# Six pairs ahead of the first gates with copied up products, and the second sequence's statistics behind the first sequence's gates

## The chip, the cores and the metric

One core of a Trainium2 chip runs the whole kernel in one launch. The metric is the device time of that launch in microseconds, lower is better, as the median of several runs.

## The reference

Eight sequences of 512 tokens go through a small language-model tower of width 128. A token's embedding is a gathered fine half and a coarse half (a softmax over 64 gathered cluster logits times a table). Then a layer norm, a linear attention with decay and a gelu memory step, each added to the residual, a second layer norm, and a mixture of 64 experts of width 64, top 6 of a softmax router, with a capacity, plus two shared experts:

```python
hg = jnp.einsum('ecd,efd->ecf', expert_in, w_gate)
hu = jnp.einsum('ecd,efd->ecf', expert_in, w_up)
expert_out = jnp.einsum('ecf,edf->ecd', jax.nn.silu(hg) * hu, w_down)
```

The kernel computes every expert for every token and multiplies each hidden row by the token's gate, which is zero where the router did not choose the expert or its capacity is used up.

## The kernel before

Experts are taken two at a time, 33 pairs a sequence (pair 0 is the shared one), as 128 hidden rows by 512 tokens. For each pair TensorE (PE) makes a gate product and an up product (three float32r matmuls each, `x_hi` and `x_lo` being the split halves of the input, `L481` to `L483`) into one of two banks each (`bank_g`, `bank_u`). ScalarE (ACT) writes `silu(gate)` into a slot of `hid` (`L623`), VectorE (DVE) multiplies the slot by the up bank (`L881`, which frees that bank), GpSimd (POOL) multiplies it by the gate rows (`L1040`, pair 0 by a constant, `L1044`), and PE adds the down product to `bank_y` (`L467`; odd pairs in three float32r matmuls, `L461` to `L464`, for which ACT makes `hid_hi`, `L629`, and DVE `hid_lo`, `L887`). `hid` has six slots, so silu of pair p waits for the down product of pair p-6.

The next sequence's attention, norm and router are cut into stages, numbered by the pair behind which they stand (`PE_AT`, `DVE_AT`, `ACT_AT`, `POOL_AT`): `late` stages prepare sequence b+1, `early` ones the embedding of b+2. Every engine's order is written out by hand, and semaphores alone tie the engines. Some stages: 0 and 1 normalise and transpose `xn` (PE `L351`), 3 and 4 make y, 5 z and scores, 6 the state (PE `L378`), 7 the memory product (PE `L386`), 8 to 12 x2, its squares and `xn2` (PE `L396`), 23 the router product (PE `L419`), 24 to 29 its softmax and top 6 on DVE, 30 the transposed gates (PE `L427`), 31 the capacity count and `gates_t` (DVE `L828`, `L833`), which SyncE (SP) stores to memory and reads back as gate rows.

The first sequence has no predecessor: its stages run alone in a prologue, with transposes of the identity (`warm`, `L512`) put in where PE would idle. The prologue also splits the weights into hi and lo parts chunk by chunk (`split_hi` on ACT, `split_lo`, `L277`, on DVE; the table `CHUNKS` holds the places, and pairs 11 on need chunk 3, "up" in `later`). `AHEAD = 3` pairs of the first sequence have their gate and up products in the prologue: pairs 0 and 1 ahead of the transposed gates, pair 2 behind them. The embedding statistics of the second sequence (`bn1`, `mv1`, `L863` to `L873`) and its inverse deviation on POOL (`inv1`, `L1021`) stand amid the first sequence's router on DVE. From then on one function per engine (`pe_sequence` and its like) runs each sequence; the stages of the second sequence stand behind the pairs 0 to 32 of the first.

Of the kernel before, what the change touches and what calls it, by code (L numbers as in the profile page):

```python
# [45 lines left out]
LAG = 4  # L46
# [42 lines left out]
def build(nc, ids, table, coarse_w, square_w, small_cols, small_rows, gate_t, up_t, down_t, out):  # L89
    ctx = ExitStack()  # L90
    with ctx:
# [114 lines left out]

        def staging(b):
            return b.rearrange("p r s -> p (r s)")[:, 0:CHUNK * P].rearrange("p (c d) -> p c d", c=CHUNK)
# [42 lines left out]
        block = ctx.enter_context(nc.Block())  # L251

# [217 lines left out]
        def gate_up(pe, b, par, p):  # L470

            q = PAIRS * b + p
            if b == 0 and p % CHUNK == 0:
                for n in ("gate", "up"):
# [18 lines left out]
        def pe_sequence(pe, b, par, late, early):  # L493
            first = b == 0
            for p in range(PAIRS):
                if p >= AHEAD or not first:
                    gate_up(pe, b, par, p)
                if p >= LAG:
                    down(pe, b, par, p - LAG)
                elif not first:  # L500
# [3 lines left out]
                if late:  # L504
                    pe_late(pe, b + 1, 1 - par, p, early)
                if early:
                    pe_early(pe, b + 2, p)
# [7 lines left out]
        def _(pe):  # L515
# [37 lines left out]
            for p in range(PAIRS):  # L553
                if p == PE_AT["gates_t"]:
                    pe.wait_ge(sem("x3_hi"), 1)
                    pe.wait_ge(sem("x3_lo"), 1)
                    for k in range(AHEAD - 1):
                        gate_up(pe, 0, 0, k)
                    warm(pe, bank_y[1], WARM_GATES)
                pe_late(pe, 0, 0, p, False)  # L560
                if p == PE_AT["gates_t"]:
                    gate_up(pe, 0, 0, AHEAD - 1)
# [72 lines left out]

        def act_sequence(act, b, par, late, early):
            first = b == 0
            for p in range(PAIRS):
                if p == ACT_AT["ffn_t"] and not first:
                    act_copy_out(act, b - 1, 1 - par)  # L640
                if late:
                    act_late(act, b + 1, 1 - par, p)
                if early:
                    act_early(act, b + 2, p)
# [3 lines left out]
                if p >= SPLIT_LAG and is_split(p - SPLIT_LAG):  # L648
# [11 lines left out]
        def _(act):  # L660
# [9 lines left out]
            for p in range(PAIRS):  # L670
                act_late(act, 0, 0, p)
                act_early(act, 1, p - SHIFT, bank_y)
                split_hi(act, p)
                if p == DOWN_HI_AT:
# [4 lines left out]
                    act.activation(gelu_sig[:, :], sig[:, :], ACT.Gelu)  # L679
            sequences(act, lambda *a: act_sequence(act, *a))  # L680
# [202 lines left out]

        def dve_lo(dve, b, par, p):
# [10 lines left out]
        def dve_sequence(dve, b, par, late, early):  # L895
            first = b == 0
            for p in range(PAIRS):
                if p == DVE_AT["result"] and not first:
                    dve_out(dve, b - 1, 1 - par)
                if late:  # L900
                    dve_late(dve, b + 1, 1 - par, p)
                if early:
                    dve_early(dve, b + 2, par, p, b // 2 + 2)
                if first:
                    split_lo(dve, PAIRS + p)
                if p >= AHEAD - 1 or not first:
                    dve_up(dve, b, par, p)
                if p >= SPLIT_LAG and is_split(p - SPLIT_LAG):
# [5 lines left out]
        def _(dve):  # L914
# [58 lines left out]
            for p in range(PAIRS):  # L973
                if p == DVE_AT["taken"]:
                    dve_up(dve, 0, 0, 0)
                dve_late(dve, 0, 0, p)
                if p == DVE_AT["taken"]:
                    dve_up(dve, 0, 0, 1)
                dve_early(dve, 1, 1, p - SHIFT, 1, bank_y)
                split_lo(dve, p)  # L980
            sequences(dve, lambda *a: dve_sequence(dve, *a))
# [42 lines left out]
        def pool_sequence(pool, b, par, late, early):  # L1024
            for p in range(PAIRS):
                if late:
                    pool_late(pool, b + 1, 1 - par, p)
                if early:
                    pool_early(pool, b + 2, p)
# [18 lines left out]
        def _(pool):  # L1048
# [74 lines left out]
```

## Time and profile before

| | |
|---|---|
| median of 3 runs | 718.56 us (717.55 to 718.6) |
| span of the profiled execution, first to last instruction | 716.0 us |
| PE busy | 692.8 us, 97% |
| DVE, POOL, ACT busy | 523.4, 466.5, 350.6 us |

The profiled execution's own time is known by its span alone; 1.6 to 2.6 us lie between that span and the runs' times. The page's slices show PE at 9 tenths or more from the ninth slice on, and below that in the first eight. A time in a row counts from the span's start. PE's matmuls overlap at their ends: the distance between two starts, not one's length, is what a matmul costs.

### The profile page before, as it was taken

Reading aid. Unit: us, or ns where it says so; the run is one execution under the profiler, and the core shown is the slowest. Engines: PE = TensorE matmul, PEld = TensorE weight load, DVE = VectorE, ACT = ScalarE, POOL = GpSimd, SP = SyncE. Lnnn points to the kernel's source line nnn. Section 1 sums busy time; section 2 is a strip of 40 time slices with the busy share of each in tenths; the row PEclk is TensorE's granted clock in tenths of the full one; section 3 lists DMA queues with packets and bytes.
Section 4 is the critical chain, followed back from the end, with each engine's and each line's share of the span. In section 5 each row is a group of like instructions: output and inputs, shape, how many; then the busy total and the mean of one; then the engine's idle time right before and its main releaser. Section 6 shows DMA issues by size and latency. Waiting matters only on the chain.

```text
span 716.0 us, 9975 instructions
## 1 busy us (share of the span) xinstructions
PE 692.8 (97%) x3133; PEld 524.7 (73%) x3133; DVE 523.4 (73%) x1074; ACT 350.6 (49%) x609; POOL 466.5 (65%) x345
## 2 busy tenths in 40 slices
PE   7788899999999999999999999999999999999998
PEld 7666677777777777777777777777777777777775
DVE  5677686987768867887769877788678766674444
ACT  3543455446454374445553474544745435534432
POOL 5035477776677767685676776676775656676664
PEclk9999999999999999999999999999999999999999
DMA  5504232243323333333333433333333433334431
GB/s 204 226 1 128 71 118 104 85 133 105 111 106 114 114 108 99 120 113 102 118 103 101 128 103 103 118 110 109 114 105 102 125 103 105 115 112 124 138 123 60
DMA packets 48869, 80.17 MB, mean 112 GB/s; under 512 B 9520, under 2 KB 13744, under 8 KB 48816
## 3 DMA queue, kind: packets, MB, share of 16 engines
q1 hardware_dynamic: 47792, 77.44, 33.4%
q0 software_dynamic: 1024, 2.10, 1.2%
q8 instruction: 25, 0.41, 0.2%
q14 instruction: 28, 0.23, 0.1%
HBM read 76.35 MB, written 3.15 MB: 111 GB/s over the span
## 4 chain that ended last, share of the span: by engine, by line
PE 88%; DVE 4%; issue 3%; POOL 2%; ACT 1%; DVEq 0%; POOLq 0%
PE bank_y L467 16%; PE bank_g L481 8%; PE bank_g L482 8%; PE bank_g L483 8%; PE bank_u L483 8%; PE bank_u L481 8%; PE bank_u L482 8%; PE bank_y L464 4%; PE bank_y L462 4%; PE bank_y L461 4%; POOL hid L1040 1%; PE bank_f L408 1%; PE bank_f L386 1%; PE bank_f L402 1%; PE bank_f L445 1%
## 5 line engine op out<-in xcount | busy, mean ns | idle before, releaser
L1040 POOL TENSOR_TENSOR hid<-hid,gate_rows 128x512 f32<-128x512 f32 x256 | 374.2, 1470 | 195.4 <-DVE hid L881 193.0
L623 ACT ACTIVATE hid<-bank_g 128x512 f32<-128x512 f32 x264 | 156.6, 599 | 264.4 <-PE bank_g L483 261.8
L881 DVE TENSOR_TENSOR hid<-hid,bank_u 128x512 f32<-128x512 f32 x264 | 178.7, 681 | 128.3 <-PE bank_u L483 78.2
L481 PE MATMUL bank_g<-x_hi,gate_hi 128*128 128x512 f32 x264 | 142.9, 541 | 0.0
L467 PE MATMUL bank_y<-hid,w_down 128*128 128x512 f32 x272 | 138.7, 591 | 0.0
L887 DVE TENSOR_TENSOR hid_lo<-hid,hid_hi 128x512 fp32r<-128x512 f32 x128 | 110.2, 861 | 2.4 <-ACT hid_hi L629 2.4
L482 PE MATMUL bank_g<-x_hi,gate_lo 128*128 128x512 f32 x264 | 104.5, 396 | 0.0
L483 PE MATMUL bank_g<-x_lo,gate_hi 128*128 128x512 f32 x264 | 104.5, 396 | 0.0
L481 PE MATMUL bank_u<-x_hi,up_hi 128*128 128x512 f32 x264 | 103.9, 393 | 0.1
L483 PE MATMUL bank_u<-x_lo,up_hi 128*128 128x512 f32 x264 | 103.8, 393 | 0.0
L482 PE MATMUL bank_u<-x_hi,up_lo 128*128 128x512 f32 x264 | 103.8, 393 | 0.0
L629 ACT ACTIVATE hid_hi<-hid 128x512 fp32r<-128x512 f32 x128 | 80.3, 628 | 5.5 <-POOL hid L1040 4.8
L481 PEld LDWEIGHTS bank_g<-x_hi,gate_hi 128*128 128x128 f32 x264 | 50.1, 190 | 24.1 <-issue 19.2
L482 PEld LDWEIGHTS bank_g<-x_hi,gate_lo 128*128 128x128 f32 x264 | 50.2, 190 | 23.9 <-issue 19.2
L467 PEld LDWEIGHTS bank_y<-hid,w_down 128*128 128x128 f32 x272 | 51.1, 188 | 11.3
L481 PEld LDWEIGHTS bank_u<-x_hi,up_hi 128*128 128x128 f32 x264 | 49.8, 189 | 12.4 <-DVE hid L881 0.6
L482 PEld LDWEIGHTS bank_u<-x_hi,up_lo 128*128 128x128 f32 x264 | 49.8, 189 | 11.8
L483 PEld LDWEIGHTS bank_g<-x_lo,gate_hi 128*128 128x128 f32 x264 | 49.7, 188 | 11.6
L483 PEld LDWEIGHTS bank_u<-x_lo,up_hi 128*128 128x128 f32 x264 | 49.8, 189 | 11.1
L461 PE MATMUL bank_y<-hid_hi,down_hi 128*128 128x512 f32 x128 | 51.3, 401 | 0.0
L464 PE MATMUL bank_y<-hid_lo,down_hi 128*128 128x512 f32 x128 | 50.8, 397 | 0.0
L462 PE MATMUL bank_y<-hid_hi,down_lo 128*128 128x512 f32 x128 | 50.6, 395 | 0.0
(209 smaller groups left out, 857.1 us busy)
## 6 DMA issues: line engine op xcount, KB each, us to landing
gate_rows<-gates_dram SPq DMA_DIRECT2D x512, 128.0 KB, 2.9
w_down<-down_t_dram SPq DMA_DIRECT2D x3, 704.0 KB, 14.5
out_dram<-later SPq DMA_DIRECT2D x7, 256.0 KB, 3.1
hid<-gate_t_dram SPq DMA_DIRECT2D x2, 704.0 KB, 5.8
gates_dram<-gates_t SPq DMA_DIRECT2D x8, 128.0 KB, 2.2
gate_rows<-up_t_dram SPq DMA_DIRECT2D x1, 704.0 KB, 5.7
later<-up_t_dram SPq DMA_DIRECT2D x1, 704.0 KB, 9.9
raw<-gate_t_dram SPq DMA_DIRECT2D x1, 704.0 KB, 11.0
```

Source lines behind the costliest of these rows:

```text
L461: pe.matmul(y, down_hi[:, j, :], hid_hi[:, k, :], start=False, stop=False)
L462: pe.matmul(y, down_lo[:, j, :], hid_hi[:, k, :], start=False, stop=False)
L464: pe.matmul(y, down_hi[:, j, :], hid_lo[:, k, :], start=False, stop=False).then_inc(sem("down_done"), 1)
L467: pe.matmul(y, w_down[:, p, :], hid[:, slot(par, p), :], start=(p == 0), stop=(p == PAIRS - 1)).then_inc(sem("down_done"), 1)
L481: pe.matmul(o, w_hi[name][:, p, :], x3_hi[par][:, :], start=True, stop=False)
L482: pe.matmul(o, w_lo[name][:, p, :], x3_hi[par][:, :], start=False, stop=False)
L483: pe.matmul(o, w_hi[name][:, p, :], x3_lo[par][:, :], start=False, stop=True).then_inc(sem("pe_" + name), 1)
L623: act.activation(hid[:, slot(par, p), :], bank_g[(p + par) % 2][:, :], ACT.Silu).then_inc(sem("silu"), 1)
L629: act.activation(hid_hi[:, (p // 2) % SPLIT_RING, :], hid[:, slot(par, p), :], ACT.Copy)\
L881: dve.tensor_tensor(hid[:, s, :], hid[:, s, :], bank_u[(p + par) % 2][:, :], ALU.mult)\
L887: dve.tensor_tensor(hid_lo[:, k, :], hid[:, slot(par, p), :], hid_hi[:, k, :].bitcast(F32), ALU.subtract)\
L1040: pool.tensor_tensor(hid[:, s, :], hid[:, s, :], gate_rows[:, row, :], ALU.mult)\
```

## The change

`AHEAD` goes to 6. The gate and up products of pairs 0 to 5 now stand ahead of the first sequence's pair loop: 0 and 1 as before, then 14 warm transposes in place of 20, pair 2, the gate product of pair 3, the transposed gates, and then the up product of pair 3 and the pairs 4 and 5. The 6 warm transposes behind the gates are gone. Since only two up banks exist, ACT copies each of these six up products to SBUF buffers that are free then (`u_copy`), and DVE multiplies silu by the copy (`dve_first_product`). The copy of pair 0 stands ahead of the router's exponential on ACT. The second sequence's `bn1` and `mv1` move on DVE from amid the router to behind the first `gates_t`; POOL gathers the third sequence's rows ahead of `inv1` and no longer behind it. The pair loop of the first sequence begins at pair 6, and three tables say which stages, down products and hi/lo splits stand behind which pair; three chunk splits on DVE move.

```diff
-AHEAD = 3
-WARM = {1: 8, 3: 12, 5: 9, 6: 7, 7: 36, 12: 3, 13: 4, 17: 24, PE_AT["gates_t"]: 6}
-WARM_START, WARM_PREP, WARM_EXP, WARM_COARSE, WARM_GATES = 20, (2, 9), 4, 26, 20
+AHEAD = 6
+FIRST_STAGES = {6: (0, 1, 2), 7: (3,), 8: (4,), 9: (5,), 10: (6,), 11: (7,), 12: (8, 9), 13: (10,), 14: (11,), 15: (12,),
+                16: (13,), 17: (14, 15), 18: (16,), 19: (17,), 20: (18,), 21: (19,), 22: (20,), 23: (21, 22), 24: (23,),
+                25: (24, 25), 26: (26,), 27: (27,), 28: (28,), 29: (29,), 30: (30,), 31: (31,), 32: (32,)}
+FIRST_DOWNS = {6: (0,), 7: (), 8: (1, 2), 9: (3, 4), 10: (5, 6)}
+FIRST_HI = {6: (1,), 7: (), 8: (3,), 9: (5,), 10: (7,)}
+FIRST_PRODUCTS = {0: (3,), 2: (4, 5)}
+WARM = {1: 8, 3: 12, 5: 9, 6: 7, 7: 36, 12: 3, 13: 4, 17: 24}
+WARM_START, WARM_PREP, WARM_EXP, WARM_COARSE, WARM_GATES = 20, (2, 9), 4, 26, 14
...
-          ("up", CHUNK, "later", None, 5, PAIRS + 5),
-          ("gate", 2 * CHUNK, "own0", None, 5, PAIRS + 9),
-          ("up", 2 * CHUNK, "own1", None, 7, PAIRS + 12))
+          ("up", CHUNK, "later", None, 5, PAIRS + 8),
+          ("gate", 2 * CHUNK, "own0", None, 5, PAIRS + 11),
+          ("up", 2 * CHUNK, "own1", None, 7, PAIRS + 13))
...
-            for name, banks, freed in (("gate", bank_g, "silu"), ("up", bank_u, "up_used")):
+            for name, banks, freed in (("gate", bank_g, "silu"),
+                                       ("up", bank_u, "u_copied" if q - 2 < AHEAD else "up_used")):
...
+        def act_copy_up(act, p):
+
+            act.wait_ge(sem("pe_up"), p + 1)
+            if p == AHEAD - 1:
+                act.wait_ge(sem("pe_coarse"), 2)
+            act.activation(u_copy[p], bank_u[p % 2][:, :], ACT.Copy).then_inc(sem("u_copied"), 1)
...
+        def dve_first_product(dve, p):
+
+            dve.wait_ge(sem("silu"), p + 1)
+            dve.wait_ge(sem("u_copied"), p + 1)
+            s = slot(0, p)
+            dve.tensor_tensor(hid[:, s, :], hid[:, s, :], u_copy[p], ALU.mult).then_inc(sem("up_used"), 1)
...
-                pool_early(pool, 1, p - SHIFT)
             for t in range(TILES):
                 gather(pool, 2, 0, t)
+            pool_early(pool, 1, POOL_AT["inv1"])
             sequences(pool, lambda *a: pool_sequence(pool, *a))
```

PE around the first sequence's transposed gates (`L427` before, `L444` in the change); gate products write `bank_g`, up products `bank_u`. Before:

```order
L512 MATMUL bank_y<-ident 128x128 x20
L427 MATMUL bank_f<-ident,turns 128x128 x4
L481 MATMUL bank_g<-x_hi,gate_hi 128x512
L482 MATMUL bank_g<-x_hi,gate_lo 128x512
L483 MATMUL bank_g<-x_lo,gate_hi 128x512
L481 MATMUL bank_u<-x_hi,up_hi 128x512
L482 MATMUL bank_u<-x_hi,up_lo 128x512
L483 MATMUL bank_u<-x_lo,up_hi 128x512
L512 MATMUL bank_y<-ident 128x128 x6
L351 MATMUL bank_f<-ident,xn 128x128 x4
```

The same place in the change:

```order
L536 MATMUL bank_y<-ident 128x128 x14
L501 MATMUL bank_g<-x_hi,gate_hi 128x512
L502 MATMUL bank_g<-x_hi,gate_lo 128x512
L503 MATMUL bank_g<-x_lo,gate_hi 128x512
L501 MATMUL bank_u<-x_hi,up_hi 128x512
L502 MATMUL bank_u<-x_hi,up_lo 128x512
L503 MATMUL bank_u<-x_lo,up_hi 128x512
L501 MATMUL bank_g<-x_hi,gate_hi 128x512
L502 MATMUL bank_g<-x_hi,gate_lo 128x512
L503 MATMUL bank_g<-x_lo,gate_hi 128x512
L444 MATMUL bank_f<-ident,turns 128x128 x4
L501 MATMUL bank_u<-x_hi,up_hi 128x512
```

Pair 2 and half of pair 3 have moved ahead of the transposed gates.

DVE from the second sequence's embedding (`L858`) into the first sequence's router (`L779` to `L789`), before:

```order
L858 TENSOR_TENSOR emb<-bank_y,soft 128x4x64
L863 BN_STATS bn<-emb 128x6 x4
L779 TENSOR_TENSOR turns<-bank_f,rows 128x256
L783 TENSOR_REDUCE rstat<-turns 128x4
L785 TENSOR_TENSOR turns<-turns,rstat 128x256
L868 BN_AGGR mv<-bn 128x2 x4
L872 TENSOR_SCALAR var<-mv 128x4
L873 TENSOR_SCALAR var<-mv 128x4
L789 TENSOR_REDUCE rstat<-turns 128x4
```

In the change the router stands there alone, and DVE has this behind the last router step (`L935` is `dve_first_product`, `L874` and `L879` the capacity count and `gates_t`, `L743` stage 0 of the second sequence):

```order
L935 TENSOR_TENSOR hid<-hid,shared 128x512
L874 SCALAR_TENSOR_TENSOR taken<-ones_row,bank_f 64x512
L879 SCALAR_TENSOR_TENSOR gates_t<-taken,bank_f 64x512
L909 BN_STATS bn<-emb 128x6 x4
L914 BN_AGGR mv<-bn 128x2 x4
L918 TENSOR_SCALAR var<-mv 128x4
L919 TENSOR_SCALAR var<-mv 128x4
L935 TENSOR_TENSOR hid<-hid,shared 128x512 x2
L743 TENSOR_SCALAR xn<-emb,mv,inv 128x128 x4
```

The eight statistics instructions and the two on the variance now follow `gates_t`; POOL's `inv1` waits for them and stands ahead of POOL's work on pair 0.

DVE around the first of the three moved chunk splits (`L277` before, `L294` in the change; `L716` and `L718` are stage 4, `L881` a product). Before:

```order
L716 TENSOR_TENSOR vo_y_lo<-bank_f,vo_y_hi 128x512
L718 TENSOR_TENSOR turns<-bank_f,decay_out 128x384
L881 TENSOR_TENSOR hid<-hid,bank_u 128x512
L703 TENSOR_SCALAR x<-emb,mv,inv 128x128 x4
L708 TENSOR_SCALAR shared<-xn,decay_cols 128x384
L277 TENSOR_TENSOR up_lo<-later,up_hi 128x1408
L881 TENSOR_TENSOR hid<-hid,bank_u 128x512
L887 TENSOR_TENSOR hid_lo<-hid,hid_hi 128x512
```

In the change (`L927` a product, the first that of pair 7; `L940` the lo half, here of pair 3):

```order
L927 TENSOR_TENSOR hid<-hid,bank_u 128x512
L762 TENSOR_TENSOR vo_y_lo<-bank_f,vo_y_hi 128x512
L764 TENSOR_TENSOR turns<-bank_f,decay_out 128x384
L294 TENSOR_TENSOR up_lo<-later,up_hi 128x1408
L927 TENSOR_TENSOR hid<-hid,bank_u 128x512
L940 TENSOR_TENSOR hid_lo<-hid,hid_hi 128x512
```

Stage 4 and the split now stand in one row ahead of the lo half of pair 3.

## Rows read from the trace of the kernel before

**Rows 1.** Windows: two stretches; length, busy us of each engine, clock, DMA.

```profile
60.70:64.10 3.40, 3.40 (x10) 2.66 (x9) 1.97 (x3) 1.52 (x3) 0.36 (x1) 0.50 0.50 153
74.40:77.80 3.40, 3.40 (x11) 3.01 (x12) 1.58 (x4) 0.50 (x2) 0.36 (x2) 0.50 0.17 62
```

**Rows 2.** Timeline of PE: start, us, what, count, idle ahead and its releaser.

```profile
50.78 2.35 PE L512 MATMUL bank_y<-ident 128*128 128x128 f32 x20
55.27 0.65 PE L427 MATMUL bank_f<-ident,turns 128*128 128x128 f32 x4 [2.14 <-DVE turns L819]
...
57.16 0.82 PE L512 MATMUL bank_y<-ident 128*128 128x128 f32 x6
59.89 0.66 PE L351 MATMUL bank_f<-ident,xn 128*128 128x128 f32 x4 [1.92 <-DVE xn L697]
...
74.36 1.62 PE L378 MATMUL bank_f<-z,shared 128*128 128x128 f32 x6 [2.24 <-issue]
```

**Rows 3.** The chain that ended last, in order of time: start, us, what.

```profile
61.16 0.43 PE bank_g L483
...
90.93 0.67 DVE xn L746 x3
...
97.04 0.86 PE bank_y L467 x2
...
99.60 0.23 PE bank_g L483
```

**Rows 4.** Timeline of DVE from the router to the pair loop.

```profile
48.24 0.87 DVE L863 BATCH_NORM_STATS2 bn<-emb 128x6 f32<-128x128 f32 x4
49.03 0.41 DVE L779 TENSOR_TENSOR turns<-bank_f,rows 128x256 f32<-128x256 f32 x1
...
50.84 0.42 DVE L789 TENSOR_REDUCE rstat<-turns 128x4 f32<-128x256 f32 x1
...
54.79 0.42 DVE L819 TENSOR_TENSOR turns<-turns 128x256 f32<-128x256 f32 x1
...
57.21 0.69 DVE L833 SCALAR_TENSOR_TENSOR gates_t<-taken,bank_f 64x512 f32<-64x512 f32 x1
...
61.82 0.68 DVE L881 TENSOR_TENSOR hid<-hid,bank_u 128x512 f32<-128x512 f32 x1
```

**Rows 5.** Timeline of ACT at the router's exponential.

```profile
50.38 0.42 ACT L607 ACTIVATE turns<-turns 128x256 f32<-128x256 f32 x1 [3.23 <-DVE turns L785]
50.82 1.28 ACT L623 ACT_TABLE_LOAD   x1
52.12 1.08 ACT L623 ACTIVATE hid<-bank_g 128x512 f32<-128x512 f32 x2
```

**Rows 6.** Timeline of POOL at the same place.

```profile
51.00 1.64 POOL L1021 TENSOR_TENSOR inv<-var,neg_half 128x8 f32<-128x8 f32 x1 [6.83 <-DVE var L873]
...
57.65 1.53 POOL L1044 TENSOR_SCALAR hid<-hid 128x512 f32<-128x512 f32 x1
```

**Rows 7.** Timeline of DVE in the first pairs.

```profile
65.72 1.15 DVE L887 TENSOR_TENSOR hid_lo<-hid,hid_hi 128x512 fp32r<-128x512 f32 x1 [2.06 <-ACT hid_hi L629]
66.80 0.68 DVE L716 TENSOR_TENSOR vo_y_lo<-bank_f,vo_y_hi 128x512 fp32r<-128x512 f32 x1
67.40 0.54 DVE L718 TENSOR_TENSOR turns<-bank_f,decay_out 128x384 f32<-128x384 f32 x1
...
70.78 1.61 DVE L277 TENSOR_TENSOR up_lo<-later,up_hi 128x1408 fp32r<-128x1408 f32 x1
```

**Rows 8.** Timeline of PE: four stages of the second sequence.

```profile
80.12 0.39 PE L386 MATMUL bank_f<-z,shared 128*128 128x128 f32 x2
...
91.70 0.61 PE L396 MATMUL bank_f<-ident,xn 128*128 128x128 f32 x4
...
119.71 1.00 PE L419 MATMUL bank_f<-cols,xn_t 128*128 128x64 f32 x8
...
135.82 0.60 PE L427 MATMUL bank_f<-ident,turns 128*128 128x128 f32 x4
```

More of the change, by code:

```diff
@@ L251, in build, with stages @@
         block = ctx.enter_context(nc.Block())
+        def stages(b, p):
+            if b:
+                return (p,)
+            return FIRST_STAGES.get(p, ())
         def alone(eng, name):
@@ L497, in pe_sequence @@
                     gate_up(pe, b, par, p)
-                if p >= LAG:
+                if first:
+                    for k in FIRST_DOWNS.get(p, (p - LAG,) if p > AHEAD else ()):
+                        down(pe, b, par, k)
+                elif p >= LAG:
                     down(pe, b, par, p - LAG)
-                elif not first:
+                else:
                     down(pe, b - 1, 1 - par, p - LAG + PAIRS)
@@ L503, in pe_sequence @@
                     pe_out(pe, b - 1)
[L504 to L507, printed above, removed]
+                for at in stages(b, p):
+                    if late:
+                        pe_late(pe, b + 1, 1 - par, at, early)
+                    if early:
+                        pe_early(pe, b + 2, at)
         def warm(pe, bank, count):
@@ L647, in act_sequence @@
                 act_silu(act, b, par, p)
-                if p >= SPLIT_LAG and is_split(p - SPLIT_LAG):
+                if first:
+                    for k in FIRST_HI.get(p, (p - SPLIT_LAG,)):
+                        if is_split(k):
+                            act_hi(act, b, par, k)
+                elif p >= SPLIT_LAG and is_split(p - SPLIT_LAG):
                     act_hi(act, b, par, p - SPLIT_LAG)
@@ L896, in dve_sequence @@
             first = b == 0
-            for p in range(PAIRS):
+            for p in range(AHEAD if first else 0, PAIRS):
                 if p == DVE_AT["result"] and not first:
                     dve_out(dve, b - 1, 1 - par)
[L900 to L903, printed above, removed]
+                for at in stages(b, p):
+                    if late:
+                        dve_late(dve, b + 1, 1 - par, at)
+                    if early:
+                        dve_early(dve, b + 2, par, at, b // 2 + 2)
+                    if first:
+                        for k in FIRST_PRODUCTS.get(at, ()):
+                            dve_first_product(dve, k)
                 if first:
                     split_lo(dve, PAIRS + p)
-                if p >= AHEAD - 1 or not first:
-                    dve_up(dve, b, par, p)
-                if p >= SPLIT_LAG and is_split(p - SPLIT_LAG):
+                dve_up(dve, b, par, p)
+                if first:
+                    for k in FIRST_HI.get(p, (p - SPLIT_LAG,)):
+                        if is_split(k):
+                            dve_lo(dve, b, par, k)
+                elif p >= SPLIT_LAG and is_split(p - SPLIT_LAG):
                     dve_lo(dve, b, par, p - SPLIT_LAG)
@@ L1025, in pool_sequence @@
             for p in range(PAIRS):
-                if late:
-                    pool_late(pool, b + 1, 1 - par, p)
+                for at in stages(b, p):
+                    if late:
+                        pool_late(pool, b + 1, 1 - par, at)
+                    if early:
+                        pool_early(pool, b + 2, at)
                 if early:
-                    pool_early(pool, b + 2, p)
                     if p in GATHER_AT and b:
```

46 lines of the change are left out of this document (32 added, 14 removed).

## The prediction

> **What bounds the kernel now.** I read the page first: PE is busy 97% of the span, and its slices are full from the ninth on. What PE loses it loses early, and since it has the same matmuls to do afterwards, what is saved or lost early shows at the end one for one. Next the timeline of PE over the prologue's end, for every stretch without pairs in it. Around the first gates PE has two holes [rows 2]. From 50.78, when pair 1 is issued, to 55.27 it has only 20 warm transposes and a wait of 2.14 us for the router's last step on DVE: 4.5 us. From 57.16 to 59.89 it has 6 warm transposes and a wait of 1.92 for the second sequence's `xn`: 2.7 us. A third wait of 2.24 us stands ahead of the state product. Then the clock: it is granted at 0.50, which is 1.2 of 2.4 GHz, in two stretches of 3.4 us, one right behind the second hole, one right behind the third [rows 1]. In them a matmul costs 0.43 us and not 0.23 [rows 3], so each stretch loses 3.4 x (1 - 0.23/0.43) = 1.6 us. Sum of before's early losses: 4.5 + 2.7 + 2.2 + 2 x 1.6 = **12.6 us**. The change can at most win these.
>
> **The change, step by step,** in the time of before's trace. PE's own costs: 0.23 us a float32r matmul, so 1.38 a pair (gate and up) and 0.69 an odd down product, and 0.86 an even one [rows 3]; four transposes 0.41 (start of `L427` to the gap-free next matmul). No row shows the new copy on ACT; the nearest is silu, also 128x512 from a bank, two in 1.08, so 0.54 each [rows 5]. It may be as short as nothing where ACT is idle.
>
> Router. Before, the four `bn1` instructions stand ahead of the router's first step, 48.24 to 49.03 [rows 4]; they go, 0.8 us. But ACT now copies pair 0's up product ahead of the exponential. That product ends near 49.5 (one pair, 1.38, ahead of 50.78, and its tail), the copy near 50.2, so the exponential begins at 50.2 and not at 50.38 [rows 5]: 0.2 are won, not 0.8. `mv1` lay in the wait for the exponential (`L789` begins 0.04 behind its end [rows 4, 5]), so its removal wins nothing. The gates are ready at 55.0, not 55.2.
>
> Before the gates PE has 14 warm transposes, by 20 in 2.3 us **1.6 us**, then pair 2's gate product, which waits for silu 0: exponential to 50.6, table load 1.28, silu 0.6 gives 52.5 [rows 5], a wait of **0.1**. Nine matmuls, to 54.6; then a wait of **0.4** for the gates, transposes to 55.45, and 21 matmuls of pairs 3 to 6, to 60.3. ACT's silu and copy, 1.08 a pair, hide beside PE's 1.38.
>
> Down product of pair 0. The moved statistics cost here. `gates_t` ended 2.63 behind the start of `L427` [rows 2, 4], so now at 57.7. Then `bn1` 0.87 and the aggregates behind it (0.7 taken, they are the shorter ones), 59.25; then POOL, whose queue holds `inv1`, 1.64, and behind it pair 0, 1.53 [rows 6]: 62.45. Queued behind POOL's wait is all of its pair work, and DVE's stage 0 waits for `inv1` too. PE stands from 60.3, **2.1 us**. Before, `inv1` was done by 52.7, off the path.
>
> Up product of pair 8. Down 0 and `xn`'s transposes end at 63.75, pair 7, y and pair 8's gate at 66.5. DVE had `x_lo` done 1.93 behind the start of `L351` [rows 2, 4], so now at 65.25; then it has the products of 4, 5 and 6, 0.6 apart: 67.05. The products of 0 to 5 now read two SBUF operands, where the old ones read a bank. An instruction with two SBUF operands that meets POOL's work took 1.15 [rows 7], against 0.68 of a product from a bank [rows 4]: with 0.47 more for two of them, 68.0. So PE waits 0.5 to 1.5. If the clock falls behind the 2.1 us, as it did behind 1.92 and 2.24, the 1.6 lost to it swallow most of that wait. I take **2.1** for both together (1.6 the one alone, 3.1 both in full).
>
> The row is one instance of that meeting. The Trainium skill, page "SBUF — State Buffer", section "SBUF: two separate sides", says of such a DVE instruction and of a GpSimd one that reads SBUF that the one that "starts first gets the pair for the whole instruction; the other fully blocks". By that rule each of the three products of this place could stand a whole POOL instruction.
>
> Down product of pair 3. Silu 7 waits for down 1's slot, then come 0.6 of silu, 0.6 of product 7, 1.06 of stage 4 (66.80 to 67.86), 1.55 of the moved chunk split, 0.6 of product 8, 0.65 of the lo half [rows 4, 7]: 5.1, and 5.6 with one meeting with POOL. PE has down 2, pair 9 and two thirds of down 3 meanwhile, 0.86 + 1.38 + 0.46 = 2.7. It waits 2.4 to 3.6, **2.9** taken, and the clock falls again, **1.6**. At down 7 the same pattern, shorter (state, product, lo half against 1.84 of PE): **0.5**.
>
> Later. The second sequence's stages now lie behind fewer pairs. From the memory product to `xn2`'s transposes PE had five pairs, 80.12 to 91.70 [rows 8], and `xn2` ended at 91.60 [rows 3]: just in time. Now there are four, 1.38 + 0.78 = 2.2 us less cover, of which the chain shrinks by at most the missing pair's product and lo half, 1.3. PE waits 0.9 to 2.2; **2.0** taken, since DVE also has two more chunk splits just ahead of it. From the router product to the transposed gates there were seven pairs, 119.71 to 135.82 [rows 8], now six; I don't know the slack from these rows, so 0 to 2.2, **1.2** taken.
>
> Sum of after's losses: 1.6 + 0.1 + 0.4 + 2.1 + 2.1 + 2.9 + 1.6 + 0.5 + 2.0 + 1.2 = **14.5 us**, against 12.6: **1.9 us slower**. The profiled span is 716.0, so 717.9 for the changed one; on the median, 718.56 + 1.9 = **720.5**. From the second sequence's own pairs on nothing is changed.
>
> **Rivals.** (a) The change wins nothing and loses nothing: the two later waits take their low ends, 0.9 and 0, since chains of stages are paced by the pairs between them. Then 14.5 - 2.3 = 12.2, a gain of 0.4: 718.2. For it: before, each such stage came just in time, as written by hand. Against it: `xn2` had no slack at all.
> (b) Faster, by the clock. It falls behind neither new hole, because PE is dense from 52.5 on but for them: 3.2 less (of which the wait at pair 8 takes back about 1), and with the low ends of (a) 12.2 - 2.2 = 10.0, a gain of 2.6: 716.0. It decides from the point where both holes stay below the 1.92 at which the clock fell before. I work them out at 2.1 and 2.9, so this is unlikely.
> (c) Slower still, by DVE and POOL meeting. If each of the three products and two of the lo halves waits a whole POOL instruction (0.47 by the row, up to the 1.15 of the whole), 5 x 0.5 = 2.5 more, of which half meets waits that are counted: 1.3 more, 721.8. By that rule of the Trainium skill, page "SBUF — State Buffer", section "SBUF: two separate sides", the time would go this way.
> (d) The change does not do what it says: pair 2 could not start ahead of the gates because silu 0 comes too late. Silu 0 would have to end behind 55; by rows 5 it ends at 52.5. Time as before.
>
> **How the numbers follow.** A measurement of this kernel tells a change from none at about 0.2%, 1.44 us: faster is below 717.1, slower above 720.0. Chances: forecast 0.50, with its own range 719.4 to 721.8 and a tenth of it below 720.0; (a) 0.25, within; (b) 0.12, of which 0.11 faster; (c) 0.10, slower; (d) 0.03, within. That gives slower 0.55, within 0.34, faster 0.11. The range reaches down to the middle of (a) and (b), 717.3, and up to 722.4, where (c) and the high ends of the waits at pairs 3 and 8 lie.
>
> **What would show it.** In the changed trace: the first hole shrunk to 14 warm transposes and less than 1 us of wait; the first even down product waiting some 2 us for POOL's pair 0, which starts right behind `inv1`; the lo product of pair 3 waiting some 3 us for DVE's lo half, with the chunk split ahead of it; two stretches at clock 0.50 between 60 and 85 us; and idle time ahead of `xn2`'s transposes, or of a gate product that waits for silu near them. The pair loop of the first sequence should be some 5 us early around pair 12 without the clock's falls and 2 with them, and late by pair 33. I am wrong if PE's waits in that stretch sum to less than before's, above all if the late ones are missing or the clock stays at 1.00.

## The result, and the profile after

The changed kernel took 721.41 us (median of 7 runs, 719.73 to 722.52), the kernel before beside it 717.92 us (7 runs, 716.48 to 718.6): a ratio of 1.005, 95% interval 1.0039 to 1.0061. It is 3.5 us slower. The forecast was 720.5, 1.9 to 2.6 us slower depending on which median of before it is set against, with a range of 717.3 to 722.4: the side and the range hold, the size is too small.

The profiled execution of the change spans 719.6 us, against 716.0. First its TensorE (PE), in the timeline: start, us, what, count, and in brackets the idle time ahead and what ended it. Left out are most of the matmuls that waited for nothing.

```profile
49.36 0.47 PE L501 MATMUL bank_g<-x_hi,gate_hi 128*128 128x512 f32 x1
...
52.17 1.69 PE L536 MATMUL bank_y<-ident 128*128 128x128 f32 x14
53.87 0.50 PE L501 MATMUL bank_g<-x_hi,gate_hi 128*128 128x512 f32 x1
...
56.38 0.66 PE L444 MATMUL bank_f<-ident,turns 128*128 128x128 f32 x4 [0.15 <-DVE turns L865]
...
64.37 2.04 PE L484 MATMUL bank_y<-hid,w_down 128*128 128x512 f32 x2 [2.52 <-POOL hid L1109]
...
71.58 0.49 PE L501 MATMUL bank_u<-x_hi,up_hi 128*128 128x512 f32 x1 [1.15 <-DVE hid L927]
...
78.98 0.50 PE L481 MATMUL bank_y<-hid_lo,down_hi 128*128 128x512 f32 x1 [2.77 <-DVE hid_lo L940]
...
87.66 0.50 PE L481 MATMUL bank_y<-hid_lo,down_hi 128*128 128x512 f32 x1 [0.51 <-DVE hid_lo L940]
...
97.57 0.50 PE L501 MATMUL bank_g<-x_hi,gate_hi 128*128 128x512 f32 x1 [0.82 <-ACT hid L651]
...
100.72 0.66 PE L413 MATMUL bank_f<-ident,xn 128*128 128x128 f32 x4 [0.76 <-DVE xn L792]
...
132.74 0.51 PE L501 MATMUL bank_u<-x_hi,up_hi 128*128 128x512 f32 x1 [0.28 <-DVE hid L927]
...
143.47 0.80 PE L501 MATMUL bank_g<-x_hi,gate_hi 128*128 128x512 f32 x1
```

The first row is pair 0, the last pair 33 (the second sequence's first). The first hole, 4.5 us before [rows 2], is 1.7 of warm transposes now, and the second, 2.7, is gone. In their place stand eight waits. In the kernel before, the same two pairs begin here:

```profile
47.98 0.47 PE L481 MATMUL bank_g<-x_hi,gate_hi 128*128 128x512 f32 x1
...
140.18 0.80 PE L481 MATMUL bank_g<-x_hi,gate_hi 128*128 128x512 f32 x1
```

So from pair 0 to pair 33 PE needed 92.20 us before and 94.11 now, 1.91 more. Pair 0 itself came 1.38 later, though PE's work ahead of it is not changed, and 0.3 came behind pair 33: 3.6 in all. Of the 1.38, 0.34 is a longer wait for the first gathered rows (2.01 us, 1.66 before), and nearly all of the rest came at half clock behind it. The windows of the change (length, busy us of PE, weight loads, DVE, ACT and POOL, granted clock, DMA share, GB/s) show the clock at half between 12.9 and 19.7, where before had the full clock. It is at half again behind the first down product, and not behind the longest wait of all, the one that ends at 78.98:

```profile
12.90:16.30 3.40, 3.34 (x15) 2.85 (x14) 0.93 (x4) 1.76 (x2) 0.68 (x1) 0.50 1.01 412
16.30:19.70 3.40, 3.40 (x18) 3.40 (x18) 3.03 (x20) 1.38 (x1) 1.68 (x1) 0.51 1.02 407
64.10:67.50 3.40, 3.13 (x8) 1.97 (x9) 0.87 (x3) 0.20 (x1) 2.53 (x3) 0.52 0.68 199
75.90:79.40 3.50, 0.73 (x4) 0.38 (x3) 3.50 (x4) 0.00 (x0) 1.34 (x2) 1.00 0.57 182
79.00:83.00 4.00, 4.00 (x22) 3.23 (x23) 4.00 (x9) 2.34 (x6) 2.14 (x2) 1.00 0.22 67
```

The fourth of these windows shows what PE waits for there: PE is busy for 0.73 of 3.50 us, VectorE (DVE) for all 3.50. Its timeline from the gates to that lo half, and one chunk split at the late waits (start, us, line, what, count; the bracket as above):

```profile
58.32 0.69 DVE L879 SCALAR_TENSOR_TENSOR gates_t<-taken,bank_f 64x512 f32<-64x512 f32 x1
58.93 0.86 DVE L909 BATCH_NORM_STATS2 bn<-emb 128x6 f32<-128x128 f32 x4
...
60.50 1.29 DVE L935 TENSOR_TENSOR hid<-hid,shared 128x512 f32<-128x512 f32 x2
62.75 1.62 DVE L743 TENSOR_SCALAR xn<-emb,mv,inv 128x128 f32<-128x128 f32 x4 [0.96 <-POOL inv L1084]
64.30 0.67 DVE L935 TENSOR_TENSOR hid<-hid,shared 128x512 f32<-128x512 f32 x1
67.94 0.69 DVE L758 TENSOR_TENSOR x_lo<-bank_f,x_hi 128x512 fp32r<-128x512 f32 x1 [2.97 <-ACT x_hi L608]
...
69.14 1.78 DVE L935 TENSOR_TENSOR hid<-hid,z 128x512 f32<-128x512 f32 x1
70.85 0.67 DVE L927 TENSOR_TENSOR hid<-hid,bank_u 128x512 f32<-128x512 f32 x1
...
73.96 0.69 DVE L927 TENSOR_TENSOR hid<-hid,bank_u 128x512 f32<-128x512 f32 x1 [1.36 <-ACT hid L651]
...
75.63 2.09 DVE L294 TENSOR_TENSOR up_lo<-later,up_hi 128x1408 fp32r<-128x1408 f32 x1
...
78.25 0.68 DVE L940 TENSOR_TENSOR hid_lo<-hid,hid_hi 128x512 fp32r<-128x512 f32 x1
...
94.28 1.62 DVE L294 TENSOR_TENSOR up_lo<-raw,up_hi 128x1408 fp32r<-128x1408 f32 x1
```

DVE is not busy all the way: it waits 2.97 us for `x_hi` and 1.36 for silu of pair 7. From 73.96 to the end of the lo half, at 78.93, its row has no gap, and that row is what PE waits for.

And POOL: `inv1`, pair 0, pairs 1 and 2, pair 3, and one at the late waits.

```profile
60.68 2.04 POOL L1084 TENSOR_TENSOR inv<-var,neg_half 128x8 f32<-128x8 f32 x1 [10.24 <-DVE var L919]
62.72 1.51 POOL L1109 TENSOR_SCALAR hid<-hid 128x512 f32<-128x512 f32 x1
65.09 2.49 POOL L1105 TENSOR_TENSOR hid<-hid,gate_rows 128x512 f32<-128x512 f32 x2 [0.87 <-DVE hid L935]
...
68.63 1.75 POOL L1105 TENSOR_TENSOR hid<-hid,gate_rows 128x512 f32<-128x512 f32 x1 [1.04 <-DMA gate_rows<-gates_dram]
...
94.44 2.58 POOL L1105 TENSOR_TENSOR hid<-hid,gate_rows 128x512 f32<-128x512 f32 x1 [1.88 <-DVE hid L927]
```

### The profile page after: what moved, and what is told of

Read it like the earlier page. It is cut to its first block, busy times and chain, and to the rows that moved or that the text cites. A ratio compares the mean times of both kernels' runs of the same rounds, so it can differ in the third digit from the quotient of the medians.

```text
span 719.6 us, 9958 instructions
## 1 busy us (share of the span) xinstructions
PE 695.2 (97%) x3121; PEld 523.6 (73%) x3121; DVE 524.1 (73%) x1074; ACT 354.1 (49%) x615; POOL 467.5 (65%) x345
## 4 chain that ended last, share of the span: by engine, by line
PE 88%; issue 4%; DVE 3%; POOL 2%; ACT 1%; DMA 1%; SPq 0%; DVEq 0%; POOLq 0%; ACTq 0%
PE bank_y L484 16%; PE bank_g L501 8%; PE bank_u L501 8%; PE bank_g L502 8%; PE bank_g L503 8%; PE bank_u L503 8%; PE bank_u L502 8%; PE bank_y L481 4%; PE bank_y L479 4%; PE bank_y L478 4%; PE bank_f L395 1%; PE bank_f L403 1%; PE bank_f L425 1%; PE bank_u L536 1%; PE bank_f L462 1%
## 5 line engine op out<-in xcount | busy, mean ns | idle before, releaser
L927 DVE TENSOR_TENSOR hid<-hid,bank_u 128x512 f32<-128x512 f32 x258 | 174.6, 681 | 125.1 <-PE bank_u L503 73.8
L501 PE MATMUL bank_g<-x_hi,gate_hi 128*128 128x512 f32 x264 | 141.0, 534 | 0.8 <-ACT hid L651 0.8
L940 DVE TENSOR_TENSOR hid_lo<-hid,hid_hi 128x512 fp32r<-128x512 f32 x128 | 108.7, 849 | 0.4 <-ACT hid_hi L657 0.4
```

The lines of the kernel that those rows point to most:

```text
L501: pe.matmul(o, w_hi[name][:, p, :], x3_hi[par][:, :], start=True, stop=False)
L927: dve.tensor_tensor(hid[:, s, :], hid[:, s, :], bank_u[(p + par) % 2][:, :], ALU.mult)\
L940: dve.tensor_tensor(hid_lo[:, k, :], hid[:, slot(par, p), :], hid_hi[:, k, :].bitcast(F32), ALU.subtract)\
```

## The experiments

How many stretches at half clock an execution has differs from run to run of one kernel. Each run has its span and its mean granted clock, and a stretch of 3.4 us at 0.50 takes 3.4 x 0.5 / 716 = 0.0024 off that mean: 0.998 or 0.997 is one such stretch, 0.995 two, 0.993 three. So beside the medians the table has the spans of the runs that had one, and of those that had none. All these kernels but the first carry 14 more warm transposes in the prologue, "three" and "six" are the pairs ahead, "early" statistics stand amid the router as before, "late" ones behind the first `gates_t` as in the change.

| kernel | median us (runs) | ratio to before, 95% | span with one stretch | with none |
|---|---|---|---|---|
| before, unchanged | 717.72 to 717.88 (81) | 1 | 714.5 to 715.3 | |
| three early, `p_before` | 718.14 (12) | 1.000 (0.999 to 1.0009) | 714.7 to 714.9 | |
| six late, `p_after` | 721.68 (6) | 1.0053 (1.0038 to 1.0068) | 718.8 (one run) | |
| six early, `p_six_early` | 719.64 (12) | 1.0028 (1.0018 to 1.0039) | 716.5 to 716.8 | |
| three late, `p_three_late` | 718.16 (11) | 1.0008 (1.0 to 1.0017) | none such, 716.0 to 716.5 with two | |
| three early, split moved, `p_three_split` | 715.25 (11) | 0.997 (0.996 to 0.9981) | 713.2 to 714.7 | |
| six early, split moved, `p_six_split` | 717.09 (12) | 0.9989 (0.9978 to 1.0001) | 715.2 to 715.5 | 713.7 to 713.8 |
| six early, late splits, `p_six_own` | 717.98 (12) | 1.0002 (0.9989 to 1.0016) | 715.2 to 715.3 | 713.7 to 713.8 |
| six early, both, `p_six_both` | 715.44 (11) | 0.9966 (0.9955 to 0.9977) | 713.5 to 713.8 | 712.3 to 712.5 |
| six late, both, `p_after_both` | 716.25 (12) | 0.9986 (0.9975 to 0.9996) | 714.0 to 714.5 | 713.8 |
| six late, POOL's order, `p_after_pool` | 719.98 (8) | 1.0036 (1.0023 to 1.005) | 717.8 to 718.3 | 717.0 |
| six early, both, products moved, `p_six_all` | 713.50 (6) | 0.9946 (0.9932 to 0.9959) | none such | 711.5 to 712.1 |
| six late, everything, `p_after_all` | 714.04 (6) | 0.9956 (0.9942 to 0.9971) | 713.6 | 712.1 to 712.3 |

### Is it the clock ahead of pair 0?

```diff
-WARM_START, WARM_PREP, WARM_EXP, WARM_COARSE, WARM_GATES = 20, (2, 9), 4, 26, 20
+WARM_START, WARM_PREP, WARM_EXP, WARM_COARSE, WARM_GATES = 20, (2, 23), 4, 26, 20
```

The kernel before with this (`p_before`):

> The kernel before with 14 more warm transposes (1.6 us) in the prologue, where TensorE waits for the first gathered rows (1.66 us of wait in the profile of before, 2.01 in the profile of the change). In the change's profile the clock fell to 0.50 right behind that wait, from 12.9 to some 19.6, and its pair 0 started 1.38 us later than before's (49.36 to 47.98), although the change touches nothing there. Theory A (the fall is a matter of when the row numbers arrive, in either kernel): with the wait filled the clock stays at 1.00 ahead of pair 0 here, the time is that of before's profile, 716.0 of span, or up to 0.7 us below before's median. Theory B (something of the change lengthens its prologue): this kernel runs as before, and the next one keeps 1.4 us behind it ahead of pair 0.

The change with it (`WARM_GATES` 14 in both of its lines; `p_after`):

> The changed kernel with the same 14 warm transposes. Theory A: pair 0 starts at 48.0, within 0.3 of the one before it here, from pair 0 to pair 33 TensorE needs 94.1 us as in the change's profile against 92.2 before, so this kernel is 1.9 to 2.2 us (0.3%) slower than the one above, and not 3.5. Theory B: 3.5 us slower, 1.4 of it ahead of pair 0.

Measured: no change to before (1.000), and the change is 3.5 us behind `p_before`, as without the warm transposes. Of theory A one half held: in both profiles the clock was full until pair 0, which began at 48.16 and 48.33. But `p_after` then fell to half at 48.2, with no idle time above 0.98 us in the 28 us ahead of it, and it was at half for most of the 3.5 us behind each of its long waits, which end at 64.65 and 78.10 (windows as above):

```profile
48.20:51.60 3.40, 3.40 (x11) 2.72 (x10) 1.61 (x5) 0.32 (x1) 0.95 (x1) 0.51 0.14 39
64.60:68.10 3.50, 3.45 (x10) 2.33 (x11) 1.08 (x3) 1.06 (x3) 2.98 (x3) 0.59 0.58 199
78.10:81.90 3.80, 3.80 (x14) 3.00 (x15) 3.46 (x7) 1.12 (x2) 1.95 (x2) 0.60 0.18 68
```

From pair 0 to pair 33 it took 95.88 us, against 92.33 of `p_before`: 3.55 more. So the 1.38 ahead of pair 0 was no part of the change, and the 1.91 behind it is not the change's size: between these two pairs the clock fell twice in the profiles of before and `p_before`, once in the change's, and three times in `p_after`'s. With one stretch each, before (714.5 to 715.3) and the change (718.5 in its first seven runs, 718.8 here) lie some 3.5 to 4 us apart.

### Statistics and pairs, one without the other

The statistics back in their old place, with six pairs ahead (`p_six_early`); the last part is on POOL:

```diff
-                if p - SHIFT < DVE_AT["bn1"]:
-                    dve_early(dve, 1, 1, p - SHIFT, 1, bank_y)
+                dve_early(dve, 1, 1, p - SHIFT, 1, bank_y)
...
-            dve_early(dve, 1, 1, DVE_AT["bn1"], 1, bank_y)
-            dve_early(dve, 1, 1, DVE_AT["mv1"], 1, bank_y)
...
+                pool_early(pool, 1, p - SHIFT)
...
-            pool_early(pool, 1, POOL_AT["inv1"])
```

> The changed kernel with the same warm transposes and with the second sequence's statistics back amid the first router, inv1 at its old place on POOL. Theory S (the moved statistics cost it): the gates come 0.8 us later, but POOL has pair 0 done by 60, so the 2.5 us wait of the first down product and the stretch at half clock behind it (1.5) go, and the later waits go along with TensorE: 94.1 - 4.2 + 0.8 = 90.7 us from pair 0 to pair 33, 3.4 us faster than the kernel above and 1.5 faster than the first. Rival C (the crowd behind six pairs ahead): what is won at the first down product comes back at the waits behind it (second sequence's xn, gate rows, up product of pair 8, lo half of pair 3), so 93 to 94 us, within 1 us of the kernel above.

The opposite edit on the kernel before (`p_three_late`):

> The kernel before with the same warm transposes, three pairs ahead, but with the second sequence's statistics behind the first gates_t and inv1 behind the third sequence's gathers, as in the change. Theory S: the gates come 0.8 us earlier, but xn waits for bn1 0.87, aggregates 0.7, inv1 1.6 to 2.0, so its transposes start 2.1 to 2.9 us later than before's 59.89, and the kernel is 2 to 3 us slower than the first. Rival C (the statistics' place is free, six pairs make the loss): up to 0.8 us faster than the first.

Measured: undoing the statistics won 2.0 us of the change's 3.5 and not 3.4; six pairs with early statistics are still slower than before. And moving them with three pairs cost nothing (718.16 to 718.14; 0.6 by the ratios, within their intervals), where a loss of 2 to 3 us was expected, the router's 0.8 already taken off. So six pairs alone, with the tables that go with them, cost 1.5 us (719.64 to 718.14), the statistics alone nothing, and both together 3.5. The hole that was to cost them is there, in PE's timeline of `p_three_late`:

```profile
63.21 1.12 PE L351 MATMUL bank_f<-ident,xn 128*128 128x128 f32 x4 [5.71 <-DVE xn L697]
...
76.42 0.91 PE L378 MATMUL bank_f<-z,shared 128*128 128x128 f32 x6
```

In `p_before` the same two are:

```profile
60.07 0.66 PE L351 MATMUL bank_f<-ident,xn 128*128 128x128 f32 x4 [1.91 <-DVE xn L697]
...
74.64 1.61 PE L378 MATMUL bank_f<-z,shared 128*128 128x128 f32 x6 [2.25 <-issue]
```

The transposes of `xn` come 3.1 us later and the state product, behind pair 6, only 1.8, because it no longer waits; pair 33 then starts 0.07 us later after pair 0. (The clock was at half there from 48 to 51 too, but PE's wait for the gates, 2.12 us in `p_before`, is gone.) What sets the state product is DVE's row up to its scores (`L725`), which starts at the lo half of pair 1. In `p_before` DVE waited 2.11 us there for `hid_hi`, which ACT makes from POOL's pair 1; in `p_three_late` that lo half comes only 1.7 later, at 67.59, and without a wait:

```profile
65.86 1.28 DVE L887 TENSOR_TENSOR hid_lo<-hid,hid_hi 128x512 fp32r<-128x512 f32 x1 [2.11 <-ACT hid_hi L629]
...
71.06 1.61 DVE L277 TENSOR_TENSOR up_lo<-later,up_hi 128x1408 fp32r<-128x1408 f32 x1
...
73.79 0.74 DVE L725 TENSOR_TENSOR shared<-bank_f,decay_mask 128x256 f32<-128x256 f32 x2
```

From 65.86 to 74.5 this row has no gap. In `p_six_early` the first down product waited for nothing, as expected. But PE then met DVE where it had met it in the change, for longer:

```profile
66.71 0.50 PE L501 MATMUL bank_u<-x_hi,up_hi 128*128 128x512 f32 x1 [1.18 <-DVE hid L927]
...
74.60 0.50 PE L481 MATMUL bank_y<-hid_lo,down_hi 128*128 128x512 f32 x1 [3.26 <-DVE hid_lo L940]
```

That gave a new theory: from the first gates to about pair 10 DVE sets the pace, and PE's waits there are one account, not several.

### Work taken out of VectorE's row

One number moves the first chunk split, 1.6 us of DVE, from behind pair 5 to the prologue, between the first `x3` and `x_lo`, where DVE had waited 1.87 us for ACT (`p_three_split`; with six pairs from `PAIRS + 8`, `p_six_split`):

```diff
-          ("up", CHUNK, "later", None, 5, PAIRS + 5),
+          ("up", CHUNK, "later", None, 5, 20),
```

> The kernel before (three pairs ahead, statistics amid the router, 14 more warm transposes in the prologue) with one thing moved: the chunk split that pairs 11 on need (up_lo from later, 1.6 to 2.1 us on VectorE) stands in the prologue, behind the first x3 and ahead of x_lo, where VectorE waited 1.87 us for ScalarE. Theory D (from the first gates to pair 10 VectorE has more to do than TensorE, so what TensorE wins or loses there is given back at the next wait for VectorE; that is why a hole of 5.7 us at xn cost nothing in the run with three pairs and late statistics): the wait ahead of the state product falls from 2.25 to some 0.7, the time by 1.5 us, to 716.3. Rival L (TensorE's waits add up one for one, each with a cause of its own): the state product waits for its own chain, at most 0.5 us change.

> Six pairs ahead, statistics amid the router, the same warm transposes, and the same chunk split in the prologue. In the run without the split moved the first down product waited for nothing, as expected, but the lo half of pair 3 waited 3.26 us where it was 2.77, and pair 33 came only 1.7 us earlier than with late statistics. Theory D: that wait falls to 0.8 to 1.2, the time by 1.5 to 2 us (more where a stretch at half clock behind it goes too), from 719.6 to some 717.8. Rival P (POOL, which then has eight pairs in a row, 12.7 us, sets the pace): the wait moves to pairs 5 and 7 and the time stays within 0.5.

Two more splits moved back by two pairs (`p_six_own`), and all three moves together (`p_six_both`):

```diff
-          ("gate", 2 * CHUNK, "own0", None, 5, PAIRS + 11),
-          ("up", 2 * CHUNK, "own1", None, 7, PAIRS + 13))
+          ("gate", 2 * CHUNK, "own0", None, 5, PAIRS + 13),
+          ("up", 2 * CHUNK, "own1", None, 7, PAIRS + 15))
```

> Six pairs ahead, statistics amid the router, the same warm transposes, and the two other chunk splits (gate_lo and up_lo from raw, 2.7 and 1.6 us on VectorE) two pairs later, behind pairs 13 and 15 and no longer 11 and 13. Theory T (the late waits are VectorE's too: the split at pair 11 holds up the residual, its squares, and so the exponential with its two table loads on ScalarE): the gate product's wait for silu at pair 15 (0.82) goes, that of xn2's transposes (0.77) halves, 1.2 to 1.8 us less, 718.1. Rival F (the second sequence's stages lie behind fewer pairs, whatever VectorE does between): both waits stay, 719.6.

> Both moves of the splits together with six pairs ahead and statistics amid the router. Theories D and T: the gains add, 3.0 to 3.5 us less than without (719.6), so 716.1 to 716.6, 1.2 to 1.7 below the kernel before. Rivals L, P, F: within 0.5 of 719.6; if only one of D and T holds, near 718.

Measured, in the medians: 2.9 us won by the one number with three pairs and 2.5 with six, where 1.5 to 2 were expected; 1.7 by the late splits; 4.2 by both. By the ratios it is 2.2, 2.8, 1.9 and 4.5. L, P and F fall; the times go with D and T. In `p_three_split` the split fits its place, and pair 0 starts as before (48.19 to 48.16):

```profile
45.45 1.62 DVE L277 TENSOR_TENSOR up_lo<-later,up_hi 128x1408 fp32r<-128x1408 f32 x1
47.40 0.69 DVE L774 TENSOR_TENSOR x_lo<-bank_f,x_hi 128x512 fp32r<-128x512 f32 x1 [0.33 <-ACT x_hi L604]
```

and PE's waits for `xn`, 1.91, and for the state product, 2.25, are these:

```profile
60.11 0.66 PE L351 MATMUL bank_f<-ident,xn 128*128 128x128 f32 x4 [0.56 <-DVE xn L697]
...
73.22 0.91 PE L378 MATMUL bank_f<-z,shared 128*128 128x128 f32 x6 [0.91 <-issue]
```

The first is not shorter by the split: `xn` ends where it did, and PE came to it later, since in this execution the clock was at half from 56.5 on. That shows how waits and clock stand in for each other. The state product's wait is shorter by 1.3, and the stretch behind it is gone; the products of `vo_y` (`L368`), ahead of it, now wait 0.65 for DVE. With one stretch each, the spans of these kernels with and without the split moved lie about 1.0 (three pairs) and 1.3 us (six) apart, so of what the medians show a third (three pairs) to a half (six) is DVE's directly, and I put the rest down to the clock. In `p_six_split` the wait for the lo half of pair 3 fell from 3.26 to 1.85, less far than the 0.8 to 1.2 expected. In `p_six_own` the gate product's wait for silu was gone, and `xn2`'s transposes waited 0.35, not 0.77.

### The changed kernel's own order

The statistics late again, with the three splits moved (`p_after_both`):

> The changed kernel, statistics behind gates_t, with the same warm transposes and both moves of the splits. So far: late against early statistics 2.0 us with the splits as in the change (721.68 to 719.64), the two moves 4.2 us with early statistics (719.64 to 715.44). Theory S (the moved statistics cost the first down product its wait, whatever VectorE does later): the gap of 2 stays, 721.7 - 4.2 = 717.5, and the first down product still waits 2.5 us. Theory D (what is lost at the first down product comes back where TensorE waits for VectorE next): the wait at the lo half of pair 3 shrinks by what the first one cost, as did the wait at the state product with three pairs, and the time is 715.4 to 716.4.

Late, splits as in the change, and only POOL's order exchanged (`p_after_pool`; the two lines move behind POOL's work on pair 0 of the first sequence):

```diff
+                    if b == 0:
+                        pool_early(pool, 1, POOL_AT["inv1"])
...
-            pool_early(pool, 1, POOL_AT["inv1"])
```

> The changed kernel with the same warm transposes and one exchange on POOL: pair 0 ahead of inv1, so that it waits for its product and no longer for inv1. The first down product's wait of 2.55 us then goes, since POOL can be done with pair 0 by some 58.5. Theory S: xn's transposes, right behind, then wait 0.7 to 1.7 us for xn, so 0.9 to 1.8 us are won, 720 to 720.8. Theory D: the wait at the lo half of pair 3 (2.77) grows by what is won, so under 0.5 us: 721.3 to 721.7.

Early, splits moved, and the products of pairs 4 and 5 ahead of `x_lo` (`p_six_all`); then the same with late statistics and POOL's exchange (`p_after_all`):

```diff
-FIRST_PRODUCTS = {0: (3,), 2: (4, 5)}
+FIRST_PRODUCTS = {0: (3, 4, 5)}
```

> Six pairs ahead, statistics amid the router, both moves of the splits, and the products of pairs 4 and 5 ahead of x_lo on VectorE (it waits there 1.60 us for x_hi) and no longer behind it. The up product of pair 8 waited 1.18 us for VectorE, behind a product that took 1.79 beside POOL. If that wait is the order's, it goes, and with theory D the lo half of pair 3 comes earlier too: 0.5 to 1.2 us less than 715.44, 714.2 to 714.9. If the products only meet POOL at another place, 715.4.

> The changed kernel, statistics behind gates_t, with everything: both moves of the splits, the products of pairs 4 and 5 ahead of x_lo, and pair 0 ahead of inv1 on POOL. Theory D: no more than 0.5 us from the run above, 714.2 to 715.4, since the gates come 0.8 us earlier and xn 0.7 to 1.7 later. Theory S: 1 to 2 us behind it, 715.5 to 717.

Measured: late statistics cost 0.8 us with the splits moved by the medians (716.25 to 715.44), 1.4 by the ratios to the runs of before on the same chip, and 2.0 or 1.8 without. In `p_after_both` the first down product still waited 2.53, but the lo half of pair 3 only 0.75 (1.83 in `p_six_both`): 716.25 lies in D's range, and by the ratio between the two.

```profile
63.40 1.10 PE L484 MATMUL bank_y<-hid,w_down 128*128 128x512 f32 x2 [2.53 <-POOL hid L1109]
...
75.10 0.50 PE L481 MATMUL bank_y<-hid_lo,down_hi 128*128 128x512 f32 x1 [0.75 <-DVE hid_lo L940]
```

From pair 0 to pair 33 PE's waits sum to 4.9 us there and to 4.5 in `p_six_both`, and pair 33 starts 89.65 and 89.56 us behind pair 0, with one stretch in each: in these profiles nearly all of the 2.53 came back. POOL's exchange won 1.7 in the medians and 1.2 by the ratios, as S had it, though the intervals overlap; with one stretch each it is 0.5 to 1.0 (718.8, one run, to 717.8 to 718.3), between the two theories. Its profile shows both parts, the wait that moved to `xn` and the one that grew from 2.77:

```profile
62.98 0.66 PE L368 MATMUL bank_f<-ident,xn 128*128 128x128 f32 x4 [1.24 <-DVE xn L743]
...
68.28 0.50 PE L501 MATMUL bank_u<-x_hi,up_hi 128*128 128x512 f32 x1 [1.50 <-DVE hid L927]
...
76.15 0.49 PE L481 MATMUL bank_y<-hid_lo,down_hi 128*128 128x512 f32 x1 [3.23 <-DVE hid_lo L940]
```

The products won more than expected, 1.4 by the ratios and 1.9 in the medians (713.50 to 715.44) for at most 1.2. In `p_six_all` they took 0.68 each (at 61.29 and 61.89), in what was DVE's idle time, and PE's longest wait between pair 0 and pair 33 is below 1 us:

```profile
71.50 0.50 PE L481 MATMUL bank_y<-hid_lo,down_hi 128*128 128x512 f32 x1 [0.76 <-DVE hid_lo L940]
...
77.00 0.50 PE L481 MATMUL bank_y<-hid_lo,down_hi 128*128 128x512 f32 x1 [0.93 <-DVE hid_lo L940]
```

All six of its runs had a mean granted clock of 0.999 or 1.000, which no run of before had. With late statistics the best is 0.5 to 0.7 us behind it, about where D had it. `p_six_all` beats both kernels: 0.54% or 4 us below before, 7 to 8 us below the change. What three pairs ahead would give with all of this was not tried.

## Why the prediction was right, and where it was not

**Side.** Right, and for the reason given: at the places it named, the waits it put there are longer than the holes they replace. (The page's slices are at 9 tenths from the sixth on, not the ninth, the middle of 718.2 and 716.0 is 717.1, not 717.3, and the 3.6 at the top of the wait at pair 3 is not worked out; the forecast's sum uses none of them.)

**The waits, place by place** (forecast, then measured from where PE's next matmul could have started). Warm transposes 1.6, 1.7. Silu of pair 0: 0.1, 0. Gates 0.4, 0.3. First down product 2.1, 2.7. Up product of pair 8, without the clock, 0.5, 1.3. Lo half of pair 3: 2.9, 2.9. At down 7: 0.5, 0.7. Late waits, silu and `xn2`: 2.0, 1.9. Router product to gates: 1.2, 0.5, and not at the gates but at an up product. That is 11.3 forecast and 12.0 measured.

**The size.** The sum of after's losses was forecast at 14.5 us, two stretches at half clock among them, and from pair 0 to pair 33 the profile has 94.11 - (92.20 - 12.6) = 14.5. That they agree is chance: the execution had one stretch there (1.6 us: the down product, transposes and first gate matmul behind its wait take 3.08 us from 64.37 to 67.45, and 0.86 + 0.41 + 0.23 = 1.5 at full clock), so its waits come to 12.9. The 0.9 beyond the 12.0 lies in small gaps that I did not assign. So the step that failed is the waits' sum, with before's 12.6 - 3.2 = 9.4: 11.3 - 9.4 = 1.9 more by the forecast, 12.9 - 9.4 = 3.5 more by the profile, and 3.5 in the medians. Of the 1.6 between them, the mis-sized terms are the first down product (0.6), the up product of pair 8 (0.8) and the small gaps (0.9), less 0.7 of the last wait.

**First down product.** The mechanism is as told, pair 0 behind `inv1` on POOL; `p_six_early` and `p_after_pool` each take the wait away. It is longer chiefly because `inv1` took 2.04 beside the two products on DVE and not the 1.64 of [rows 6], beside router steps.

**Up product of pair 8.** I priced DVE and POOL meeting at 0.47 for two products, by the 1.15 of [rows 7]. One of them took 1.78, against the 0.67 of pair 3's, so it stood nearly a whole POOL instruction: POOL's ran from 68.63 to 70.38, and DVE's, issued at 69.14, ended at 70.92, 0.54 behind it. The rule of the Trainium skill, page "SBUF — State Buffer", section "SBUF: two separate sides", that of a DVE instruction with two SBUF operands and a GpSimd one that reads SBUF the one that starts second is blocked until the first has ended, says that. The trace agrees from the other side as well: POOL's instruction at 94.44 took 2.58 where two took 2.49, while a split of DVE's ran from 94.28 to 95.90; 95.90 + 1.25 = 97.15, and it ended at 97.02. The product of pair 6, which reads a bank, took 0.67 at 70.85 with POOL busy beside it. So the forecast's "each of the three products" was one too many, since only those of pairs 4 and 5 have both operands in SBUF; and of these two one was held up. (c) was the better price for that one; as an outcome it gave 721.8, close to what was measured, but only 0.8 us of the excess lies at this place. `p_six_all` shows that with the same operands another place in DVE's order avoids the meeting.

**"What is saved or lost early shows at the end one for one."** This first step of mine is wrong. Taken as a statement on the total it must hold, but I used it for each hole by itself. `p_three_late` has a hole of 5.71 for one of 1.91, and its time is the same; `p_six_early` took away a wait of 2.55 us at the first down product and won 2.0 at the end; late statistics cost 0, about 1 or 2 us depending on what DVE has to do behind them. I had worked out DVE's row ahead of the lo half of pair 3 (5.1 us, 5.6 with one meeting; it took 5.6, from silu 7 at 73.33) and did not ask what it means that the same row stands ahead of before's state product: DVE, 73% busy by the page, is the bound of that stretch, and PE, 97% busy, is not.

**Late waits.** Right in size, wrong in the main cause. I put them on fewer pairs behind the stages. `p_six_own` kept the stages and moved two splits: the wait for silu went, that of `xn2` halved. I had named the splits in half a sentence and given them no price.

**Clock.** Forecast at two stretches for each kernel. The runs of before have 1 to 4 (29 of 81 have one, 32 three), the change's seven 1 to 4 as well. Rival (b) put its deciding point at a hole of 1.92 us; but a wait of 2.77 was followed by half clock in `p_after` and by full clock in the change's profile. The hole's length alone doesn't decide, so that point was not one. Before's own rows had said so: behind its wait of 2.14 us [rows 2] the six matmuls of pair 2 took 0.25 us each, which is full clock. What holds is the coarse reading: of `p_six_all`, in whose profile all of PE's waits behind pair 0 are under 1 us, none of six runs had such a stretch. Of the two stretches that were to lie between 60 and 85 us, the change's profile has one and `p_after`'s two. Pair 12 began 1.3 us early in the change's profile (40.11 us behind pair 0, 41.39 before) where 2 were forecast with the clock's falls, and pair 33 came late, as forecast.

**(d)** is out: pair 2 starts at 53.87 without a wait.

## What to carry to other kernels

Where a mostly busy engine waits several times in one stretch, look for one dense row of another engine behind all these waits; then closing a hole on the first engine may only make the next wait longer: here 2.5 to 3.8 us of a wait were worth 0 to 2.0 us at the end. The test is cheap: move one piece of independent work out of that row into a measured idle place of the same engine, here 1.6 us by one number, worth 2.5 to 2.9 us. Issuing more pairs ahead had not paid even then: with the splits moved, six pairs stand level with three (715.44 to 715.25). Six were ahead only with the products that belong to them put where DVE had time (713.50), and what three pairs could still win is not shown.

## What the runs showed of the hardware

How many stretches at half clock an execution has differs between runs of one program (1 to 4 in before's), and which wait is followed by one differs between programs as near as the change and `p_after`. A fall can come without a long wait: `p_after` fell at 48.2 with nothing above 0.98 us idle in the 28 us ahead of it. One kernel's runs so spread over 2 to 3 us, and a difference of 1.9 us between two profiles stood for one of 3.5 in the medians. Spans compared at the same mean granted clock agree better: before's 29 runs with one stretch lie within 0.8 us. The mean alone does not settle it, though: at 0.995 before's spans go from 714.9 to 716.9.

A DVE instruction with two SBUF operands that met POOL's cost more than I had expected in both directions: 1.11 us on a product of 0.67, 1.33 on POOL's 1.25, and 0.4 on `inv1`, which has only 8 columns, beside two products. A product with one operand from a bank took its 0.67 beside POOL all the same.
